# Local attention: values projected over 128 tokens and routed through DRAM as rows

## The chip, the cores and the metric

The kernel runs on one core of one Trainium2 chip. The metric is the device time of one execution in microseconds (us). Inside the core, TensorE (PE) multiplies matrices, VectorE (DVE), ScalarE (ACT) and GpSimd (POOL) work element by element, and SyncE (SP) issues the transfers (DMAs) that 16 DMA engines carry out. The core's on-chip memory has 128 partitions; TensorE writes its results into PSUM, eight banks of 128 x 512 float32.

## The reference, cut to what matters

The program computes two gated blocks on 4 sequences of 1024 tokens with 128 channels. The change touches the last part, six layers of local attention with a feed-forward net behind each:

```python
DIM = 128; DEPTH = 6; HEADS = 16; DIM_HEAD = 64; WINDOW = 32
def attn_layer(x, Wqkv, qs, ksc, Wo):
    q, k, v = jnp.split(x @ Wqkv, 3, -1)          # 16 heads of 64 channels each
    q = l2norm(q) * qs; k = l2norm(k) * ksc
    q, k = rotated and scaled by position
    # the queries of a window of 32 tokens see the keys and the values of
    # their own window and of the one before: 64 tokens, masked to a band
    sim  = einsum('bhwie,bhwje->bhwij', bq, bk2) * 8.0
    out  = einsum('bhwij,bhwje->bhwie', softmax(masked sim), bv2)
    return out @ Wo
for i in range(DEPTH):
    x = attn_layer(shift_tokens(x), ...) + x
    x = ffn_layer(shift_tokens(x), ...) + x
```

All of it is float32. What matters for the change is `bv2`: each window of 32 queries is multiplied with 64 rows of values, the window's own 32 and the 32 ahead of them, so the ranges of 64 tokens overlap by half.

## The kernel before, in words

The tokens of all sequences form 32 tiles of 128 tokens (`NT` = 32, `P` = 128). The function `layers` holds all six layers in one block, in which each engine has its own program and waits on semaphores. `reach(eng, l, sem, n)` waits for the n-th event of layer l.

Each engine walks through the tiles by `steps(...)`: in step n it does the listed pieces of work, each for tile n minus its lateness. On TensorE the order within one step is: queries of tile n (`make_q`, L1610), keys of tile n (`make_k`, L1623), transposed queries of tile n-1 (`turn_q`, L1631), 12 of the 16 output projections of tile n-3 (`project`, L1710), transposed keys of tile n-1 (`turn_k`, L1642), the other 4 projections (`project_rest`), transposed probabilities of tile n-2 (`turn_p`, L1653), scores of tile n-1 (`score`, L1662 for the mask and L1671), values of tile n (`make_v`, L1684) and the weighted sum of values of tile n-2 (`weigh`, L1703). So the values of tile n are used two steps after they are made. Each float32 matmul appears in the trace as two matmuls with two weight loads.

Values before: `make_v` projects each tile in four matmuls, two per half of the tile (64 tokens each), whose results stand in the lower and in the upper 64 columns of the array: the even heads of a token lie in partitions 0 to 63 and the odd ones in partitions 64 to 127. ScalarE copies them to `values` (`out_v`, L1834), two slots per tile in a ring of three tiles (`RING` = 3). That gives the windows that begin at a multiple of 64 tokens. The windows in between are put together in a second ring, `mixed`: SyncE copies blocks of 32 partitions within the on-chip memory, 4 transfers of 128 KB per tile, or 6 where the ring wraps (L1580 to L1585). `weigh` waits for them by `mixes`, then takes `mixed` and `values` in turn, window by window, in matmuls on 64 rows and 64 columns of the array with 32 moving columns.

At the start of the block GpSimd clears two stretches of memory (L2057, L2058), and TensorE and SyncE wait for that. The small weights of the net are fetched at the start of a layer (L1573), those of the next layer's attention at its end (L1592).

Of the kernel before, what the change touches and what calls it, by code (L numbers as in the profile page):

```python
# [8 lines left out]
ACT = mybir.ActivationFunctionType  # L9
AX_X = mybir.AxisListType.X  # L10
F32 = mybir.dt.float32
# [3 lines left out]
P = 128  # L15
# [3 lines left out]
T = B * L  # L19
CH = 512  # L20
NCH = T // CH
NT = T // P
# [20 lines left out]
DH = 64  # L43
INNER = HEADS * DH
PAIRS = HEADS // 2
PAIRS_AHEAD = 6
WIN = 32
# [51 lines left out]
def chunk(c):  # L99
    return slice(c * CH, (c + 1) * CH)  # L100
# [1332 lines left out]


AHEAD_TILES = 3
RING = 3
VALUE_SLOT, SCORE_SLOT, KEY_SLOT, OUT_SLOT = range(4)


# [10 lines left out]
FETCHES, NEXT = 4, 4  # L1450


def layers(nc, ps, k, w, xs, cur, fetches, w1, w2, b1, small, next_fetches):

# [21 lines left out]
    with Stage(nc, "layer") as st:  # L1476
# [7 lines left out]
        prob = st.sb("prob", [P, PAIRS, 2, DH])  # L1484
        prob_t = st.sb("prob_t", [P, PAIRS, P])
        top, total = st.sb("top", [P, HEADS]), st.sb("total", [P, 2, HEADS])
        values = st.sb("values", [P, 2 * RING, PAIRS, DH])
        mixed = st.sb("mixed", [P, 2 * RING, PAIRS, DH])
        heads_out = st.sb("heads_out", [P, PAIRS, P])

        fetched, cleared, mixes = st.sem("fetched"), st.sem("cleared"), [st.sem(f"mixes{r}") for r in range(RING)]
# [13 lines left out]
        two_banks = lambda slot: ps[:, 2 * slot:2 * slot + 2, :]  # L1505
# [28 lines left out]
        for sem, n in (  # L1534
                (fetched, 16 * FETCHES), (next_in, 16 * NEXT), (q_made, NT), (k_made, NT), (v_made, NT), (q_turned, NT),
                (k_turned, NT), (scored, NT), (p_turned, NT), (weighed, NT), (projected, NT), (q_squared, NT), (k_squared, NT),
                (logged, NT), (q_out, NT), (k_out, NT), (raised, NT), (p_out, NT), (o_out, NT), (v_out, NT), (q_parts, 2 * NT),
                (k_parts, 2 * NT), (summed, 2 * NT), (guarded, NT), (inverted, NT), (topped, NT), (shifted, NT), (totalled, NT),
                (evened, NT), (over, NT), (added, NT), (q_rotated, 2 * NT), (k_rotated, 2 * NT), (q_scaled, NT), (k_scaled, NT),
                (lows, 2 * NCH), (ups, 2 * NCH), (turned, NCH), (summed_up, NCH), (centres, NCH), (squared, NCH), (spread, NCH),  # L1540
                (norm_evened, 3), (norm_logged, 3), (norm_inverted, 3), (norm_scaled, NCH), (backs, NCH), (outs, NCH),
                (lefts, len(units)), (gates, len(units)), (gelus, len(units)), (gated, len(units)), (net_summed, len(units)),
                (done, NCH), (roped, 4), *((mixes[r], 16 * (4 if r else 6) * len(range(r, NT, RING))) for r in range(RING))):
            per_layer[id(sem)] = n

        def reach(eng, l, sem, n):

            n += l * per_layer[id(sem)]
            if n > 0:
                eng.wait_ge(sem, n)  # L1550
# [2 lines left out]

            return lambda t: do() if t == NT - 1 else None

        def mix_count(t):
            return 16 * (4 if t % RING else 6) * (t // RING + 1)

        def steps(*plan):
            for n in range(NT + AHEAD_TILES):  # L1560
# [4 lines left out]
        with nc.Block() as block:  # L1565

            @block.sync
            def _(sp):
                sp.wait_ge(cleared, 2)
                for l in range(LAYERS):  # L1570
                    reach(sp, l, done, 0)
                    for dst, src in fetches(l):
                        sp.dma_start(dst, src).then_inc(fetched, 16)  # L1573
                    for t in range(NT):
                        r = t % RING * 2
                        reach(sp, l, v_out, t + 1)
                        reach(sp, l, weighed, t - RING + 1)
                        for lo in (0, DH):
                            a, b = slice(lo, lo + WIN), slice(lo + WIN, lo + DH)
                            sp.dma_start(mixed[b, r:r + 2], values[a, r:r + 2]).then_inc(mixes[t % RING], 16)  # L1580
                            if r:
                                sp.dma_start(mixed[a, r:r + 2], values[b, r - 1:r + 1]).then_inc(mixes[t % RING], 16)
                            else:
                                sp.dma_start(mixed[a, 1], values[b, 0]).then_inc(mixes[t % RING], 16)
                                sp.dma_start(mixed[a, 0], values[b, 2 * RING - 1]).then_inc(mixes[t % RING], 16)  # L1585
                    for t in range(NT - RING, NT):
                        reach(sp, l, mixes[t % RING], mix_count(t))
                    reach(sp, l, fetched, 16 * FETCHES)
                    reach(sp, l, projected, NT)
                    if l + 1 < LAYERS:  # L1590
                        for to, of in next_fetches(l + 1):
                            sp.dma_start(to, of).then_inc(next_in, 16)  # L1592
                        reach(sp, l, next_in, 16 * NEXT)

            @block.tensor
            def _(pe):
# [78 lines left out]
                def make_v(t):  # L1675
                    if t >= 2:
                        reach(pe, l, p_out, t - 1)
                    else:
                        reach(pe, l, q_out, t)
                    if t == 0 and l:  # L1680
                        reach(pe, l, gelus, 0)
                    for a in range(2):
                        for h in range(2):
                            last = nc.tensor.matmul(two_banks(VALUE_SLOT)[h * DH:(h + 1) * DH, a, :],  # L1684
                                                    xs[:, t * P + a * DH:t * P + (a + 1) * DH],
                                                    w["qkv"][:, 2, chunk(h)], start=True, stop=True)
                    last.then_inc(v_made, 1)

                def weigh(t):
                    reach(pe, l, p_out, t + 1)  # L1690
                    reach(pe, l, mixes[t % RING], mix_count(t))
                    if t + 2 < NT:
                        reach(pe, l, k_parts, 2 * t + 6)
                    else:
                        reach(pe, l, o_out, t)
                    for p in range(0, PAIRS, 2):
                        for i in range(P // WIN):
                            src = (mixed, values)[i % 2]
                            for h in range(2):
                                for e in range(2):  # L1700
                                    rows, at = slice(h * DH, (h + 1) * DH), slice(e * DH, (e + 1) * DH)
                                    out = by_pair(KEY_SLOT)[at, h * 4 + p // 2, i * WIN:(i + 1) * WIN]
                                    last = nc.tensor.matmul(out, src[rows, t % RING * 2 + i // 2, p + e, :],  # L1703
                                                            prob_t[rows, p + e, i * WIN:(i + 1) * WIN],
                                                            start=True, stop=True)
                    last.then_inc(weighed, 1)
# [78 lines left out]
            def _(act):  # L1785
# [252 lines left out]
            def _(pool):  # L2038
# [92 lines left out]
def build_program(nc, a, out):  # L2131


    with ExitStack() as whole:
# [3 lines left out]
        def loads(tensors):  # L2138
# [52 lines left out]
        with ExitStack() as ctx:  # L2191
# [7 lines left out]
            def for_attention(layer):  # L2199
# [3 lines left out]
            shift_tokens(nc, cur, xs, w["rope"], w["scales"])  # L2203
            layers(nc, ps, k, w, xs, cur, lambda l: [(t[:], a[n][l]) for n, t in (("w1", w1), ("w2", w2), ("b1", b1),
                                                                                  ("small", small))],
                   w1, w2, b1, small, for_attention)
        gate_and_store(nc, ps, x, s, cur, out)


# [107 lines left out]
```

## Time and profile before

| What | Value |
|---|---|
| median of 3 runs | 4994.56 us (4994.17 to 4994.9) |
| profiled execution | 5013.37 us, of which the span from first to last instruction is 5011.6 us |
| granted TensorE clock, mean | 0.951 of full speed |
| busy share of the span | PE 89%, DVE 74%, ACT 55%, POOL 43% |
| DMA over the span | 204.72 MB, mean 41 GB/s |

A profile shows one execution. Each engine's busy time is the time in which it works on recorded instructions. The span is cut in 40 slices, whose digits show the busy share in tenths. A timeline lists instructions in order of their start; neighbours of one kind are merged, so that a line's time runs to the end of the last of them, and a bracket names the idle time before a line and what ended it. "issue" stands there for a wait for which the trace has no cause.

### The profile page before, as it was taken

How to read it: one execution, taken by the hardware profiler on the slowest of the kernel's cores; microseconds unless marked ns; L12 is line 12 of the kernel's file. 1: busy time of each engine (PE TensorE's matmuls, PEld its weight loads, DVE VectorE, ACT ScalarE, POOL GpSimd, SP SyncE). 2: the span in 40 equal slices, each digit the busy share in tenths (PEclk: the TensorE clock that was granted, in tenths of full speed). 3: DMA queues.
4: the chain of work that ended last, by engine and by line, in shares of the span. 5: the costliest groups of instructions: out<-in, count | busy, mean ns of one | idle time of the engine just before them, and what ended most of it. 6: DMA issues, size and time to landing. Idle time of an engine off the chain costs nothing. (4 is left out here: it accounts for less than half of the span.)

```text
span 5011.6 us, 169931 instructions
## 1 busy us (share of the span) xinstructions
PE 4437.7 (89%) x75610; PEld 2774.2 (55%) x75610; DVE 3689.3 (74%) x4181; ACT 2775.2 (55%) x3767; POOL 2162.7 (43%) x1739
## 2 busy tenths in 40 slices
PE   2876888595898699999999999999999999999998
PEld 1652333363333267765777476756776577646774
DVE  1667887124788488877888688858987799768885
ACT  1644777233677555655665565655655566545664
POOL 1332000313000066645665466636664566546661
PEclk6997999696999899999999999999999999999999
DMA  1002111112011111111111111111111111111110
GB/s 42 1 25 66 39 45 33 60 36 84 25 43 41 54 40 41 41 49 31 41 41 37 44 41 41 41 44 39 41 39 49 36 41 41 38 42 41 39 40 25
DMA packets 108209, 204.72 MB, mean 41 GB/s; under 512 B 28594, under 2 KB 56882, under 8 KB 105650
## 3 DMA queue, kind: packets, MB, share of 16 engines
q1 hardware_dynamic: 105432, 189.65, 14.5%
q8 instruction: 598, 9.80, 0.8%
q0 software_dynamic: 2048, 4.20, 0.3%
q14 instruction: 131, 1.07, 0.1%
HBM read 67.52 MB, written 22.81 MB: 18 GB/s over the span
## 5 line engine op out<-in xcount | busy, mean ns | idle before, releaser
L2044 POOL TENSOR_TENSOR part_of_layer<-part_of_layer,sine_of_layer 128x512 f32<-128x512 f32 x768 | 963.2, 1276 | 620.7 <-DVE sine_of_layer L1920 620.7
L2055 POOL TENSOR_TENSOR part_of_layer<-part_of_layer,inverse_of_layer 128x1024 f32<-128x1024 f32 x384 | 730.1, 1901 | 261.2 <-ACT inverse_of_layer L1803 246.1
L976 ACT ACTIVATE prob_of_ca<-ps 128x1024 f32<-128x1024 f32 (+3 forms) x768 | 591.9, 814 | 245.4 <-PE ps L850 173.0
L1917 DVE TENSOR_TENSOR part_of_layer<-ps,rope 128x1024 f32<-128x1024 f32 x384 | 466.1, 1214 | 33.0 <-ACT square_of_layer L1791 31.4
L1920 DVE TENSOR_TENSOR sine_of_layer<-ps,rope 128x1024 f32<-128x1024 f32 x384 | 464.8, 1210 | 0.0
L1834 ACT ACTIVATE values_of_layer<-ps 128x1024 f32<-128x1024 f32 x192 | 196.5, 1023 | 458.4 <-PE ps L1684 458.4
L868 PE MATMUL ps<-keys_of_ca,queries_of_ca 64*128 64x512 bf16 (+3 forms) x1536 | 325.8, 341 | 133.9 <-DVE top_of_ca L1008 59.7
L1703 PEld LDWEIGHTS ps<-prob_t_of_layer,mixed_of_layer 64*64 64x64 f32 x12288 | 342.4, 135 | 164.1 <-issue 154.5
L1710 PE MATMUL ps<-heads_out_of_layer,wo 128*128 128x128 f32 x3072 | 417.8, 281 | 13.1 <-ACT heads_out_of_layer L1823 12.1
L1956 DVE TENSOR_REDUCE total_of_layer<-prob_of_layer 128x16 f32<-128x1024 f32 x192 | 234.1, 1219 | 237.9 <-ACT prob_of_layer L1827 237.9
L1610 PE MATMUL ps<-qkv,shifted 128*128 128x512 f32 x768 | 383.2, 621 | 24.0 <-POOL values_of_layer L2058 19.9
L1703 PE MATMUL ps<-prob_t_of_layer,mixed_of_layer 64*64 64x32 f32 x12288 | 392.7, 221 | 13.0 <-ACT prob_t_of_layer L1818 6.7
L1703 PE MATMUL ps<-prob_t_of_layer,values_of_layer 64*64 64x32 f32 x12288 | 391.0, 220 | 12.9 <-issue 12.0
L1710 PEld LDWEIGHTS ps<-heads_out_of_layer,wo 128*128 128x128 f32 x3072 | 383.4, 197 | 16.9 <-ACT heads_out_of_layer L1823 16.9
L1684 PE MATMUL ps<-qkv,shifted 128*64 128x512 f32 x1536 | 383.7, 612 | 7.1 <-issue 7.1
L1008 DVE TENSOR_REDUCE top_of_ca<-ps 128x2 f32<-128x1024 f32 (+1 forms) x320 | 357.3, 1117 | 40.2 <-PE ps L868 24.8
L1623 PE MATMUL ps<-qkv,shifted 128*128 128x512 f32 x768 | 362.8, 595 | 12.0 <-DVE sine_of_layer L1920 12.0
L1703 PEld LDWEIGHTS ps<-prob_t_of_layer,values_of_layer 64*64 64x64 f32 x12288 | 345.2, 135 | 18.8 <-issue 17.4
L1813 ACT ACTIVATE keys_of_layer<-ps 128x1024 f32<-128x1024 f32 x192 | 196.8, 1025 | 248.9 <-PE ps L1642 248.9
L919 PE MATMUL ps<-prob_of_ca,values_of_ca 128*32 128x512 f32 (+3 forms) x3072 | 327.2, 498 | 0.7 <-ACT summed_of_ca L962 0.7
L1964 DVE TENSOR_TENSOR prob_of_layer<-prob_of_layer,total_of_layer 128x1024 f32<-128x1024 f32 x192 | 318.4, 1658 | 6.6
L1671 PE MATMUL ps<-keys_of_layer,queries_of_layer 64*32 64x64 f32 x24576 | 298.7, 228 | 4.1 <-issue 3.2
(237 smaller groups left out, 8831.1 us busy)
## 6 DMA issues: line engine op xcount, KB each, us to landing
mixed_of_layer<-values_of_layer SPq DMA_DIRECT2D x636, 128.0 KB
mixed_of_layer<-values_of_layer SPq DMA_DIRECT2D x264, 64.0 KB
queries_of_ca<-q_parts SPq DMA_DIRECT2D x384, 32.0 KB
keys_of_ca<-k_parts SPq DMA_DIRECT2D x384, 32.0 KB
qkv<-in_qkv SPq DMA_DIRECT2D x6, 1536.0 KB, 6.3
q_parts<-parts_of_ci SPq DMA_DIRECT2D x16, 384.0 KB, 2.5
k_parts<-parts_of_ci SPq DMA_DIRECT2D x16, 384.0 KB
rope<-in_rope SPq DMA_DIRECT2D x6, 1024.0 KB, 8.9
```

The source lines that it names most:

```text
L919: last = nc.tensor.matmul(ps[h * QUAD:(h + 1) * QUAD, SUM_BANK, j:], values[:, G % 2, kt, h, :], prob[:, i % 2, h, j:], start=kt == 0, sto ...
L976: nc.scalar.activation(prob[:, i % 2, 2 * two:2 * two + 2, j:], ps[:, 2 * two:2 * two + 2, j:], ACT.Exp, scale=scale).then_inc(raised, 1)
L1008: nc.vector.reduce_max(to, pair[:, :, 0:width], AX_X).then_inc(pair_used, 1)
L1610: last = nc.tensor.matmul(two_banks(SCORE_SLOT)[:, a, :], xs[:, tokens(t)], w["qkv"][:, 0, chunk(a)], start=True, stop=True)
L1623: last = nc.tensor.matmul(two_banks(KEY_SLOT)[:, a, :], xs[:, tokens(t)], w["qkv"][:, 1, chunk(a)], start=True, stop=True)
L1684: last = nc.tensor.matmul(two_banks(VALUE_SLOT)[h * DH:(h + 1) * DH, a, :], xs[:, t * P + a * DH:t * P + (a + 1) * DH], w["qkv"][:, 2, chu ...
L1703: last = nc.tensor.matmul(out, src[rows, t % RING * 2 + i // 2, p + e, :], prob_t[rows, p + e, i * WIN:(i + 1) * WIN], start=True, stop=True)
L1710: last = nc.tensor.matmul(two_banks(OUT_SLOT)[:, 0, 0:P], w["o"][:, p, :], heads_out[:, p, :], start=p == 0, stop=p == PAIRS - 1)
L1917: nc.vector.tensor_tensor(part[:, t % 2, side], by_head(slot), table(2 * side, t), ALU.mult).then_inc(parts, 1)
L1920: nc.vector.tensor_tensor(sine[:, side], by_head(slot), table(2 * side + 1, t), ALU.mult).then_inc(parts, 1)
L2044: nc.gpsimd.tensor_tensor(out, out, sine[:, side, :, (1 - to) * half:(2 - to) * half], ALU.add).then_inc(rotated, 1)
L2055: nc.gpsimd.tensor_tensor(part[:, t % 2, side], part[:, t % 2, side], by, ALU.mult).then_inc(scaled, 1)
```

## The change

`make_v` projects the 128 tokens of a tile at once, in two matmuls with all 128 columns, as `make_k` does. The results (token by row) go to `values`, now two slots of one tile. SyncE writes each tile as 128 rows of 4 KB (512 KB) to a new DRAM tensor `v_rows`, which begins with 32 rows of zeros, waits until it has landed, and then reads the four overlapping ranges of 64 tokens of that tile back, in four transfers of 256 KB (two per parity of the heads, two per parity of the window), into `windows`, a ring of two tiles. `weigh` reads all four windows from there. The matmuls of `weigh` keep their number and shape.

```diff
-RING = 3
+RING = 2
...
-        values = st.sb("values", [P, 2 * RING, PAIRS, DH])
-        mixed = st.sb("mixed", [P, 2 * RING, PAIRS, DH])
+        values = st.sb("values", [P, 2, 2, PAIRS * DH])
+        windows = st.sb("windows", [P, RING, P // WIN, PAIRS, DH])
...
             def _(sp):
                 sp.wait_ge(cleared, 2)
+                sp.dma_start(v_rows[0:WIN, :], values[0:WIN, 1].rearrange("p h n -> p (h n)")).then_inc(padded, 16)
+                sp.wait_ge(padded, 16)
...
                     for t in range(NT):
-                        r = t % RING * 2
                         reach(sp, l, v_out, t + 1)
+                        sp.dma_start(v_rows[WIN + t * P:WIN + (t + 1) * P, :], values[:, t % 2].rearrange("p h n -> p (h n)"))\
+                            .then_inc(stored[t % 2], 16)
+                        reach(sp, l, stored[t % 2], stores(t))
                         reach(sp, l, weighed, t - RING + 1)
-                        for lo in (0, DH):
-                            a, b = slice(lo, lo + WIN), slice(lo + WIN, lo + DH)
-                            sp.dma_start(mixed[b, r:r + 2], values[a, r:r + 2]).then_inc(mixes[t % RING], 16)
-                            if r:
-                                sp.dma_start(mixed[a, r:r + 2], values[b, r - 1:r + 1]).then_inc(mixes[t % RING], 16)
-                            else:
-                                sp.dma_start(mixed[a, 1], values[b, 0]).then_inc(mixes[t % RING], 16)
-                                sp.dma_start(mixed[a, 0], values[b, 2 * RING - 1]).then_inc(mixes[t % RING], 16)
+                        for h in range(2):
+                            for odd in range(2):
+                                of = v_rows[t * P + odd * WIN:(t + 1) * P + odd * WIN, h * CH:(h + 1) * CH]
+                                sp.dma_start(windows[h * DH:(h + 1) * DH, t % RING, odd::2].rearrange("r a p d -> r a (p d)"),
+                                             of.rearrange("(a r) n -> r a n", r=DH)).then_inc(windowed[t % RING], 16)
...
-                    for a in range(2):
-                        for h in range(2):
-                            last = nc.tensor.matmul(two_banks(VALUE_SLOT)[h * DH:(h + 1) * DH, a, :],
-                                                    xs[:, t * P + a * DH:t * P + (a + 1) * DH],
-                                                    w["qkv"][:, 2, chunk(h)], start=True, stop=True)
+                    for h in range(2):
+                        last = nc.tensor.matmul(two_banks(VALUE_SLOT)[:, h, :], xs[:, tokens(t)],
+                                                w["qkv"][:, 2, chunk(h)], start=True, stop=True)
                     last.then_inc(v_made, 1)
...
-                    reach(pe, l, mixes[t % RING], mix_count(t))
+                    reach(pe, l, windowed[t % RING], window_count(t))
...
-                            src = (mixed, values)[i % 2]
...
-                                    last = nc.tensor.matmul(out, src[rows, t % RING * 2 + i // 2, p + e, :],
+                                    last = nc.tensor.matmul(out, windows[rows, t % RING, i, p + e, :],
...
                 def out_v(t):
                     reach(act, l, v_made, t + 1)
-                    reach(act, l, weighed, t - RING + 1)
-                    if t >= RING - 1:
-                        reach(act, l, mixes[(t + 1) % RING], mix_count(t - RING + 1))
-                    nc.scalar.activation(values[:, t % RING * 2:t % RING * 2 + 2], by_head(VALUE_SLOT).rearrange(
-                        "p (a h) d -> p a h d", a=2), ACT.Copy).then_inc(v_out, 1)
+                    if t < 2:
+                        act.wait_ge(padded, 16)
+                    if t >= 2 or l:
+                        reach(act, l, stored[t % 2], stores(t - 2))
+                    nc.scalar.activation(values[:, t % 2], two_banks(VALUE_SLOT), ACT.Copy).then_inc(v_out, 1)
...
-                nc.gpsimd.memset(values[:, 2 * RING - 1], 0.0).then_inc(cleared, 1)
+                nc.gpsimd.memset(values[:, 1], 0.0).then_inc(cleared, 1)
...
+        v_rows = nc.dram_tensor("v_rows", [WIN + T, INNER], F32).ap()
```

## Rows read from the trace of the kernel before

**Rows 1.** The page: TensorE's busy share and granted clock in 40 slices.

```profile
PE   2876888595898699999999999999999999999998
...
PEclk6997999696999899999999999999999999999999
```

**Rows 2.** Windows: stretch, then busy us (instructions) per engine, granted clock, DMA share, GB/s.

```profile
2300.00:2740.00 440.00, 429.17 (x9805) 304.77 (x9813) 386.34 (x369) 260.75 (x317) 292.10 (x226) 0.99 0.18 41
...
3390.00:3830.00 440.00, 431.15 (x9919) 306.97 (x9915) 389.36 (x372) 261.54 (x315) 285.16 (x220) 1.00 0.17 40
```

**Rows 3.** Timeline of PE, one step: start us, us, engine, line, instructions.

```profile
2012.63 1.99 PE L1610 MATMUL ps<-qkv,shifted 128*128 128x512 f32 x4
2014.46 1.88 PE L1623 MATMUL ps<-qkv,shifted 128*128 128x512 f32 x4
2016.17 1.04 PE L1631 MATMUL ps<-sb_ident,part_of_layer 128*128 128x128 f32 x8
...
2021.01 1.49 PE L1671 MATMUL ps<-keys_of_layer,queries_of_layer 64*32 64x64 f32 x128
2022.42 1.94 PE L1684 MATMUL ps<-qkv,shifted 128*64 128x512 f32 x8
2024.29 0.32 PE L1703 MATMUL ps<-prob_t_of_layer,mixed_of_layer 64*64 64x32 f32 x8
...
2026.29 1.98 PE L1610 MATMUL ps<-qkv,shifted 128*128 128x512 f32 x4
```

**Rows 4.** Timeline of PE: the longest stalls inside a step.

```profile
4306.34 1.48 PE L1671 MATMUL ps<-keys_of_layer,queries_of_layer 64*32 64x64 f32 x128
4309.35 1.94 PE L1684 MATMUL ps<-qkv,shifted 128*64 128x512 f32 x8 [1.53 <-issue]
```

**Rows 5.** The page: DMA queues with packets, MB, share of 16 engines.

```profile
q1 hardware_dynamic: 105432, 189.65, 14.5%
q8 instruction: 598, 9.80, 0.8%
```

**Rows 6.** Timeline of PE's weight loads (PEld): values, then queries.

```profile
2008.69 0.20 PEld L1684 LDWEIGHTS ps<-qkv,shifted 128*64 128x64 f32 x4
2009.17 0.14 PEld L1684 LDWEIGHTS ps<-qkv,shifted 128*64 128x64 f32 x2 [0.29 <-issue]
2009.60 0.14 PEld L1684 LDWEIGHTS ps<-qkv,shifted 128*64 128x64 f32 x2 [0.29 <-issue]
2010.56 0.21 PEld L1703 LDWEIGHTS ps<-prob_t_of_layer,mixed_of_layer 64*64 64x64 f32 x8 [0.81 <-issue]
...
2012.63 0.30 PEld L1610 LDWEIGHTS ps<-qkv,shifted 128*128 128x128 f32 x2
2013.17 0.19 PEld L1610 LDWEIGHTS ps<-qkv,shifted 128*128 128x128 f32 x1 [0.24 <-issue]
```

**Rows 7.** Timeline of SP's queue: the issues of one tile.

```profile
2012.92 0.59 SPq L1585 DMA_DIRECT2D mixed_of_layer<-values_of_layer  x1
2013.55 0.59 SPq L1580 DMA_DIRECT2D mixed_of_layer<-values_of_layer  x1
```

**Rows 8.** DMA issues: operation, count, KB each, median us from issue to landing.

```profile
qkv<-in_qkv SPq DMA_DIRECT2D x6, 1536.0 KB, 6.3
q_parts<-parts_of_ci SPq DMA_DIRECT2D x16, 384.0 KB, 2.5
rope<-in_rope SPq DMA_DIRECT2D x6, 1024.0 KB, 8.9
```

**Rows 9.** Timelines of ACT and PE: the last tile of a layer.

```profile
2191.99 1.02 ACT L1834 ACTIVATE values_of_layer<-ps 128x1024 f32<-128x1024 f32 x1 [2.23 <-PE ps L1684]
...
2212.94 0.32 PE L1703 MATMUL ps<-prob_t_of_layer,mixed_of_layer 64*64 64x32 f32 x8 [1.11 <-ACT prob_t_of_layer L1818]
```

**Rows 10.** Windows: loads from DRAM, then the `mixed` transfers of one tile.

```profile
2219.00:2229.00 10.00, 8.55 (x31) 4.50 (x32) 5.55 (x9) 6.57 (x10) 2.77 (x4) 1.00 0.83 321
2011.70:2017.50 5.80, 5.80 (x85) 3.80 (x78) 4.62 (x5) 4.12 (x5) 4.15 (x3) 1.00 0.36 82
```

**Rows 11.** Timelines of POOL and PE: the start of the layers.

```profile
1746.18 0.52 POOL L2058 MEMSET values_of_layer<- 128x512 f32 x1
...
1746.76 3.78 PE L1610 MATMUL ps<-qkv,shifted 128*128 128x512 f32 x4 [19.89 <-POOL values_of_layer L2058]
```

More of the change, by code:

```diff
@@ L1450, with layers @@
 FETCHES, NEXT = 4, 4
-def layers(nc, ps, k, w, xs, cur, fetches, w1, w2, b1, small, next_fetches):
+def layers(nc, ps, k, w, xs, cur, fetches, w1, w2, b1, small, next_fetches, v_rows):
     units = [(c, f) for c in range(NCH) for f in range(NCHUNKS)]
@@ L1486, in layers @@
         top, total = st.sb("top", [P, HEADS]), st.sb("total", [P, 2, HEADS])
-        values = st.sb("values", [P, 2 * RING, PAIRS, DH])
-        mixed = st.sb("mixed", [P, 2 * RING, PAIRS, DH])
+        values = st.sb("values", [P, 2, 2, PAIRS * DH])
+        windows = st.sb("windows", [P, RING, P // WIN, PAIRS, DH])
         heads_out = st.sb("heads_out", [P, PAIRS, P])
-        fetched, cleared, mixes = st.sem("fetched"), st.sem("cleared"), [st.sem(f"mixes{r}") for r in range(RING)]
+        fetched, cleared, padded = st.sem("fetched"), st.sem("cleared"), st.sem("padded")
+        stored, windowed = [st.sem(f"stored{r}") for r in range(2)], [st.sem(f"windowed{r}") for r in range(RING)]
         q_made, k_made, v_made = st.sem("q_made"), st.sem("k_made"), st.sem("v_made")
@@ L1542, in layers @@
                 (lefts, len(units)), (gates, len(units)), (gelus, len(units)), (gated, len(units)), (net_summed, len(units)),
-                (done, NCH), (roped, 4), *((mixes[r], 16 * (4 if r else 6) * len(range(r, NT, RING))) for r in range(RING))):
+                (done, NCH), (roped, 4), *((stored[r], 16 * NT // 2) for r in range(2)),
+                *((windowed[r], 16 * 4 * len(range(r, NT, RING))) for r in range(RING))):
             per_layer[id(sem)] = n
@@ L1554, in last, with stores, window_count @@
             return lambda t: do() if t == NT - 1 else None
-        def mix_count(t):
-            return 16 * (4 if t % RING else 6) * (t // RING + 1)
+        def stores(t):
+            return 16 * (t // 2 + 1)
+        def window_count(t):
+            return 16 * 4 * (t // RING + 1)
         def steps(*plan):
@@ L1574, in _ @@
                     for t in range(NT):
-                        r = t % RING * 2
                         reach(sp, l, v_out, t + 1)
+                        sp.dma_start(v_rows[WIN + t * P:WIN + (t + 1) * P, :], values[:, t % 2].rearrange("p h n -> p (h n)"))\
+                            .then_inc(stored[t % 2], 16)
+                        reach(sp, l, stored[t % 2], stores(t))
                         reach(sp, l, weighed, t - RING + 1)
-                        for lo in (0, DH):
-                            a, b = slice(lo, lo + WIN), slice(lo + WIN, lo + DH)
-                            sp.dma_start(mixed[b, r:r + 2], values[a, r:r + 2]).then_inc(mixes[t % RING], 16)
-                            if r:
-                                sp.dma_start(mixed[a, r:r + 2], values[b, r - 1:r + 1]).then_inc(mixes[t % RING], 16)
-                            else:
-                                sp.dma_start(mixed[a, 1], values[b, 0]).then_inc(mixes[t % RING], 16)
-                                sp.dma_start(mixed[a, 0], values[b, 2 * RING - 1]).then_inc(mixes[t % RING], 16)
+                        for h in range(2):
[3 more added lines that the diff above has]
+                                             of.rearrange("(a r) n -> r a n", r=DH)).then_inc(windowed[t % RING], 16)
                     for t in range(NT - RING, NT):
-                        reach(sp, l, mixes[t % RING], mix_count(t))
+                        reach(sp, l, windowed[t % RING], window_count(t))
                     reach(sp, l, fetched, 16 * FETCHES)
@@ L2205, in build_program @@
                                                                                   ("small", small))],
-                   w1, w2, b1, small, for_attention)
+                   w1, w2, b1, small, for_attention, v_rows)
         gate_and_store(nc, ps, x, s, cur, out)
```

## The prediction

> **What bounds the kernel now.** I read the page first, for who is busy and where. From about slice 15 on, the six layers, TensorE stands at 9 in almost every slice, at nearly full granted clock [rows 1]. Next come the windows of single layers: in 440 us TensorE is busy 429 to 431 us, VectorE 386 to 389 us, the DMA engines 17 to 18% of the time [rows 2]. So TensorE sets the pace of these 3,200 us, with VectorE at 88% behind it, and transfers have room. The number of matmuls gives the length of a step: the listed loops make 320 recorded matmuls per tile (8 for queries and keys, 24 for the transposes, 16 projections, 8 for the mask, 128 scores, 8 values, 128 weighing), so 9,805 to 9,919 in 440 us are 30.6 to 31.0 tiles, 14.2 to 14.4 us each.
>
> The timeline of TensorE shows one step from inside. From one start of L1610 to the next it takes 13.66 us, and each group begins when the one before lets it [rows 3]. Nothing in it waits for values. What separates the usual 14.2 to 14.4 us from 13.66 us are stalls such as the 1.53 us after a block of scores, which the trace puts down to no engine ("issue") [rows 4]. About 0.6 us per tile, 192 tiles: 115 us in all. TensorE's instructions come by DMA too: 598 packets of 9.80 MB on the queue marked instruction [rows 5], 16.4 KB each, which is one for 250 or so of the 151,220 matmuls and weight loads, 2.5 per tile. They are what I suspect behind these stalls.
>
> **The value projection on TensorE.** Before, it costs 1.87 us from its start to the start of L1703, 192 times [rows 3]. The loads show the inside [rows 6]: the first pair of half-width matmuls takes 0.48 us (2008.69 to 2009.17), the next ones 0.43 us each, and the last pair, which begins one interval after 2009.60, gives way to L1703 only after 0.53 us, at 2010.56. Two half-width matmuls run side by side, so that four of them cost no more streaming time than two of full width: halving the count saves nothing there. What differs is entry and exit. The full-width queries, which too follow a group of small matmuls, pay 0.54 us for the first matmul (2012.63 to 2013.17), since a load of 128 columns takes 0.19 us where one of 64 takes 0.14 us, and then 0.43 us each. The exit stays: L1703 still has another array shape. The sum after is 0.54 + 0.43 + 0.43 + 0.53 = 1.93 us, against 1.87 us: +0.06 us from these rounded rows. I take 0.055 us x 192 = **+10.5 us**. Bounds: down to -29 us if the values then cost what the keys cost between two full-width groups, 1.71 us [rows 3] ((1.71 - 1.87) x 192 = -31 us, taken as the end), and up to +16 us if draining 128 columns takes 0.03 us more than draining 64 (half of the 0.06 us by which entries differ).
>
> The Trainium skill says the same of the exit in TensorEngine Tiling (Array Packing), section Key Properties: changing the tiling mode drains the array. By it the 0.10 us at the exit remain with full-width values, and -29 us is out of reach; the trace agrees in that both switches next to the values cost something, 0.05 and 0.10 us.
>
> Does TensorE's extra time reach the end? Its step is a chain without idle time [rows 3], and the work that hangs on the values (ScalarE's copy, the exponentials behind it, VectorE's sums) starts from the same moment as `weigh` and moves along. So all of it counts. The 8 fewer entries of 640 in TensorE's stream also cut 1% of its instruction packets: -1 us of 115 us of stalls.
>
> **The transfers.** Removed per tile: 4 or 6 issues of 0.59 us on SyncE [rows 7], 512 KB. Added: one store of 512 KB, a wait for it, four reads of 256 KB; 1.5 MB together. By rows: a store of 384 KB lands 2.5 us after its issue [rows 8], so 512 KB in some 2.8 us; then four issues of about 0.6 us [rows 7], the last at 2.8 + 1.8 = 4.6 us, and at most 6.3 us for it, the time of a load of 1.5 MB, or 8.9 us, that of 1 MB behind 2 MB of others [rows 8]. The windows of a tile are there 11 to 13.5 us after its copy. They are needed two steps later, 26 us in the middle of a layer; the shortest notice is the last tile's, from 2193.01 (2191.99 + 1.02) to 2212.94, 19.9 us [rows 9]. Margin: over 6 us at the worst point. SyncE itself is held for 2.8 + 2.4 = 5.2 us of 13.7 us. Behind its new wait stand only the same tile's reads and the next tile's store, which comes a step later; `weighed` of tile t-2 is done at about the time at which tile t's values are copied, before the store lands. ScalarE's new wait is for the store of two tiles ago. The cover is 6 us wide; if it were gone, every microsecond beyond would be paid on `weigh`, at first once per layer.
>
> Capacity: loads from DRAM ran at 321 GB/s with the engines 83% busy, the on-chip `mixed` transfers at 82 GB/s with 36% [rows 10]; per full share that is 387 and 228 GB/s. So 1.57 MB take 4.1 to 6.9 us of each step, a share of 0.30 to 0.50 after 0.17. No bound, but instruction packets share the engines. Their mean time now is 0.8% x 16 x 5011.6 us / 598 = 1.07 us [rows 5]. If a packet is held in proportion to the added share (0.13 to 0.33), it is 0.14 to 0.35 us late. TensorE runs through instructions fast only in the scores and in weighing, and of a step the new transfers cover the time from the copy to 8 to 11 us on; the copy of the tile in [rows 3] ends at about 2022.42 + 1.94 + 1.02 = 2025.4, the next scores begin one step after 2021.01, at 2034.7, 9 us later. So I see a part of one packet per tile touched, a tenth of the stall time at 0.14 us: 192 x 0.1 x 0.14 = 3 us. Bounds: 0, if no packet that TensorE waits for meets a read, and 27 us, if one in each tile does. I take **+3 us**.
>
> The Trainium skill, in Runtime: NRT & Kernel Launch, section Instruction fetch mechanics, has the fetches "mostly hidden". By it this term would be 0; the stalls of [rows 4] speak against that here.
>
> **The start.** GpSimd clears 1,024 elements per partition in place of 512, which took 0.52 us, and TensorE waits for it [rows 11]: **+0.5 us**. SyncE's write of the zeros and the wait for it (under 3 us by the 2.5 us above) lie ahead of small loads that the net needs only at the layer's end, and ScalarE's first copy of values waits for TensorE's first projections, of which the queries alone take 3.78 us there [rows 11]: nothing.
>
> **Sum.** 10.5 + 3 + 0.5 - 1 = +13 us on the profiled execution's 5013.37 us, 0.26%. That execution is 18.8 us above the median of the runs (4994.56 us); the added work is the same in both. So 4994.56 + 13: **5007.5 us**. Rounding to 0.01 us alone moves the main term by 2 us either way.
>
> **The rivals.**
> 1. *No change that can be measured* (within 0.2%, 10 us, about what a measurement of this kernel can tell from no change). The same mechanism with the entry at 0.04 us or less and untouched packets: +5 to +9 us, 5002 us. For it: the rows' second digit. Against it: three of the four terms are positive. Chance 0.34 for all sums from -10 to +10 us.
> 2. *Instruction packets held by the reads.* The bytes triple, and the stalls are real [rows 4]. If each tile has one packet 0.14 us late on top of the main term: +27 + 10 = 5032 us; at 0.35 us, 5070 us. Against it: most of the new traffic lies under long matmuls, and `mixed` was slower per byte. Chance 0.14.
> 3. *Faster: the switch costs vanish.* If the 0.10 us at the exit belong to the half-width form and not to L1703's, values cost 0.54 + 3 x 0.43 = 1.83 us, the queries' price: (1.83 - 1.87) x 192 = -8 us; with the keys' 1.71 us, 4966 us. It decides for faster once the values cost less than 1.81 us. Chance 0.08.
> 4. *The windows come late.* If write, wait and read took over 20 us, each layer's end would be held, over 26 us every tile; at 30 us 4 us for each second tile or so, some 384 us, 5380 us. Rows give 13.5 us at most. Chance 0.03.
> 5. The forecast, +10 to +25 us: 0.41.
>
> **How the numbers follow.** Slower by over 0.2% (above 5004.5 us): forecast, packets and late windows, 0.41 + 0.14 + 0.03 = 0.58. Same: 0.34. Faster: 0.08. The range leaves out rival 3 below -8 us and, above, the upper half of rival 2 and rival 4: 4987 to 5030 us. The likeliest case alone: 5004.5 to 5020 us.
>
> **What would show it.** In the changed profile, the step from the start of the value projection to L1703 should be 1.91 to 1.94 us, with 4 matmuls of 128*128; the waits of L1703 should name no DMA; a tile's last read should land within 14 us of the copy; the DMA share of a layer should be 0.30 to 0.50; and the issue stalls before L1671, L1684 and L1703 should keep their sums within 20 us. The prediction is wrong if the value group takes 1.83 us or less, if stalls grow by 30 us or more, or if `weigh` is seen waiting for `windows`.

## The result, and the profile after

The changed kernel takes 5271.82 us (median of 4 runs, 5256.11 to 5283.99) against 4994.73 us (median of 4): a ratio of 1.055, 95% interval 1.052 to 1.0581, or 277 us more. The profiled execution took 5256.11 us with a span of 5254.3 us, 243 us more than the profiled execution of before (5013.37 us). The forecast was +13 us.

The page of the changed kernel: TensorE's busy share and granted clock, the DMA engines' share, and the queues (compare [rows 1] and [rows 5]).

```profile
PE   2977887777897799889999899999999899899998
...
PEclk6998998787999899999999999999999999999998
DMA  1011111112111444424342344324342344423431
...
q1 hardware_dynamic: 200520, 391.11, 28.1%
q8 instruction: 592, 9.70, 0.8%
```

TensorE is no longer at 9 in every slice of the layers. DMA bytes doubled, and the engines' share went from 14.5% to 28.1%. The same 430 us of the first layer, which hold steps alone in both kernels, before and then after (columns as in [rows 2]):

```profile
1760.00:2190.00 430.00, 419.12 (x9610) 297.20 (x9608) 381.49 (x364) 255.88 (x310) 286.71 (x224) 1.00 0.18 41
```

```profile
1760.00:2190.00 430.00, 395.49 (x8813) 283.20 (x8813) 342.23 (x333) 232.79 (x282) 258.17 (x201) 0.97 0.41 104
```

TensorE is busy 24 us less, at a mean granted clock of 0.97 after 1.00. With 320 recorded matmuls per tile before and 316 after, the step has grown from 14.3 to 15.4 us.

The timeline of all engines shows where the time goes, in one step (start us, us, engine, line; the bracket is idle time and its end):

```profile
2017.89 2.53 SPq L1590 DMA_DIRECT2D windows_of_layer<-v_rows  x4
...
2022.58 1.40 PE L1677 MATMUL ps<-keys_of_layer,queries_of_layer 64*32 64x64 f32 x118
...
2026.94 0.45 PE L1677 MATMUL ps<-keys_of_layer,queries_of_layer 64*32 64x64 f32 x10 [2.96 <-issue]
...
2027.32 3.78 PE L1689 MATMUL ps<-qkv,shifted 128*128 128x512 f32 x4
...
2031.13 1.02 ACT L1838 ACTIVATE values_of_layer<-ps 128x1024 f32<-128x1024 f32 x1 [7.38 <-PE ps L1689]
```

After 118 of 128 score matmuls TensorE stops for 2.96 us, though it needs no new data: the other ten belong to the same group. Then the value projection takes 3.78 us in place of the 1.98 us that four matmuls of this shape take at full clock [rows 3]. The windows of single microseconds around it show both reasons (busy us per engine, granted clock, DMA share, GB/s; a DMA packet is counted where it starts, so that a share can be over 1):

```profile
2020.00:2021.00 1.00, 1.00 (x12) 1.00 (x11) 1.00 (x2) 0.00 (x0) 1.00 (x1) 1.00 1.10 279
2021.00:2022.00 1.00, 1.00 (x11) 1.00 (x11) 1.00 (x2) 0.97 (x1) 1.00 (x2) 1.00 1.06 199
2022.00:2023.00 1.00, 1.00 (x52) 0.60 (x53) 1.00 (x2) 0.70 (x2) 0.69 (x2) 1.00 1.07 229
2023.00:2024.00 1.00, 0.98 (x92) 0.82 (x84) 1.00 (x2) 0.72 (x3) 0.10 (x1) 1.00 1.04 199
2024.00:2025.00 1.00, 0.00 (x0) 0.00 (x0) 0.29 (x1) 0.00 (x0) 1.00 (x1) 1.00 0.18 31
2025.00:2026.00 1.00, 0.00 (x0) 0.00 (x0) 0.00 (x0) 0.00 (x0) 1.00 (x2) 1.00 0.00 0
2026.00:2027.00 1.00, 0.06 (x5) 0.06 (x10) 0.00 (x0) 0.00 (x0) 1.00 (x2) 0.62 0.00 0
2027.00:2028.00 1.00, 1.00 (x11) 0.64 (x12) 0.54 (x1) 0.00 (x0) 1.00 (x2) 0.50 0.00 0
```

From 2020 to 2024 the DMA engines are full with the four reads. In the microsecond in which they end, 31 KB move, then nothing. The DMA queues show what came behind the reads (packets, MB, share of 16 engines), first for 2014.90 to 2024.20, then for 2024.20 to 2024.24:

```profile
q1 hardware_dynamic: 634, 1.24, 57.0%
q14 instruction: 1, 0.01, 0.4%
```

```profile
q8 instruction: 1, 0.02, 228.0%
q1 hardware_dynamic: 4, 0.00, 11.1%
```

q8 brings TensorE's instructions: before, 598 packets for 151,220 matmuls and weight loads [rows 5], now 592 for 149,684, and 1,536 fewer entries in 6 fewer packets are 256 per packet (the last experiment, which takes back the projection alone, has 598 packets again). In the first stretch, 9.3 us long, none of its packets starts. The next one starts at the moment at which the reads end. It takes 228% x 16 x 0.04 = 1.46 us, until 2025.7, and TensorE goes on at 2026.94, 1.3 us behind it and 2.7 us after the reads ended.

This is no single case. The trace's packet records, set beside TensorE's matmuls, have 87 stalls of over 1 us inside a group of scores or of weighing. Each ends 1.05 to 1.55 us (median 1.41 us) after an instruction packet has ended, and in 68 of the 87 that packet started when at most 20 of the 512 pieces of the tile's reads had still to start. In the other runs, and in the one such stall of the kernel before, the time from the packet's end is 1.2 to 1.8 us. When a packet is asked for, the trace does not tell.

Within the 3 us of idle time the granted clock goes to the lower level (0.5 is 1.2 GHz), at 2026.2, and it stays there for 13.7 us: the matmuls that follow run at half rate.

Over the whole execution, the list of waits (engine, line, what it waited for: us in total, times, longest) has

```profile
PE ps L1677 <- issue: 166.7, 86, 3.1
...
PE ps L1706 <- issue: 38.6, 45, 3.1
```

Before, the same two lines read 3.2 us in 10 waits and 17.6 us in 36:

```profile
PE ps L1703 <- issue: 17.6, 36, 1.1
...
PE ps L1671 <- issue: 3.2, 10, 0.5
```

So 184.5 us of new idle time stand in plain sight in scores and weighing. Both lists are of profiled executions, which differ by 243 us, so 58 us are left. The clock can hold them: its mean over the execution is 0.936 after 0.951, and (1 - 0.936) x 5254.3 - (1 - 0.951) x 5011.6 = 91 us of full-rate work, a part of which falls into the idle time itself.

### The profile page after: what moved, and what is told of

Its sections match the earlier page's. It is cut to its first block and busy times, and to the rows that moved or that the text cites. A ratio compares the mean times of both kernels' runs of the same rounds, so it can differ in the third digit from the quotient of the medians.

```text
span 5254.3 us, 168459 instructions
## 1 busy us (share of the span) xinstructions
PE 4510.1 (86%) x74842; PEld 2845.4 (54%) x74842; DVE 3662.7 (70%) x4181; ACT 2775.7 (53%) x3767; POOL 2149.7 (41%) x1739
## 3 DMA queue, kind: packets, MB, share of 16 engines
q1 hardware_dynamic: 200520, 391.11, 28.1%
## 5 line engine op out<-in xcount | busy, mean ns | idle before, releaser
L1706 PEld LDWEIGHTS ps<-prob_t_of_layer,windows_of_layer 64*64 64x64 f32 x24576 | 401.7, 139 | 204.4 <-issue 194.9
L1706 PE MATMUL ps<-prob_t_of_layer,windows_of_layer 64*64 64x32 f32 x24576 | 429.7, 223 | 46.2 <-issue 38.6
L1677 PE MATMUL ps<-keys_of_layer,queries_of_layer 64*32 64x64 f32 x24576 | 313.6, 229 | 166.7 <-issue 166.7
L1689 PE MATMUL ps<-qkv,shifted 128*128 128x512 f32 x768 | 429.5, 686 | 7.9 <-issue 7.9
L1616 PE MATMUL ps<-qkv,shifted 128*128 128x512 f32 x768 | 390.6, 631 | 25.8 <-POOL values_of_layer L2061 20.8
L1946 DVE TENSOR_REDUCE top_of_layer<-ps 128x16 f32<-128x1024 f32 x192 | 235.0, 1224 | 228.3 <-PE ps L1677 228.3
L1677 PEld LDWEIGHTS ps<-keys_of_layer,queries_of_layer 64*32 64x32 f32 x24576 | 266.3, 107 | 223.6 <-issue 223.3
L1629 PE MATMUL ps<-qkv,shifted 128*128 128x512 f32 x768 | 364.2, 597 | 14.9 <-DVE sine_of_layer L1923 14.9
L1967 DVE TENSOR_TENSOR prob_of_layer<-prob_of_layer,total_of_layer 128x1024 f32<-128x1024 f32 x192 | 282.7, 1472 | 6.6
```

The lines of the kernel that those rows point to most:

```text
L1616: last = nc.tensor.matmul(two_banks(SCORE_SLOT)[:, a, :], xs[:, tokens(t)], w["qkv"][:, 0, chunk(a)], start=True, stop=True)
L1629: last = nc.tensor.matmul(two_banks(KEY_SLOT)[:, a, :], xs[:, tokens(t)], w["qkv"][:, 1, chunk(a)], start=True, stop=True)
L1677: last = nc.tensor.matmul(out, queries[rows, p, i * WIN:(i + 1) * WIN], keys[rows, p, first:first + DH], start=False, stop=p == PAIRS - 1)
L1689: last = nc.tensor.matmul(two_banks(VALUE_SLOT)[:, h, :], xs[:, tokens(t)], w["qkv"][:, 2, chunk(h)], start=True, stop=True)
L1706: last = nc.tensor.matmul(out, windows[rows, t % RING, i, p + e, :], prob_t[rows, p + e, i * WIN:(i + 1) * WIN], start=True, stop=True)
```

## The experiments

Theory A: TensorE's instruction packets stand behind the window reads on the DMA engines, and what it costs depends on where in the step the traffic lies. The rivals: B, the full-width projection disturbs TensorE; C, the new waits cost; D, the added bytes slow the core wherever they lie. Each ratio is to the kernel before, run on the same chip; there the kernel before took 5023.8 us beside the first four experiments and 5016.9 and 5010.9 us beside the others (medians). The changed kernel was not run again beside them; the last experiment, at 1.0564, comes nearest to it. The edits are shown shortened.

### The projection alone

```diff
 kernel before
-  matmul(two_banks(VALUE_SLOT)[h * DH:(h + 1) * DH, a, :], xs[:, t * P + a * DH:t * P + (a + 1) * DH], ...)  # x4
+  matmul(two_banks(VALUE_SLOT)[:, h, :], xs[:, tokens(t)], w["qkv"][:, 2, chunk(h)])                         # x2
```

> The kernel before with the full-width value projection alone (two matmuls with 128 columns in place of four with 64); the values then stand in another order than the weighing takes them for, so the attention output is another one. Theory A (TensorE's instruction packets stand behind the window reads on the DMA engines): this part costs only what the prediction gave it, about +10 us, 5005 us (5000 to 5012), and the granted clock in the layers stays near 1.0. Theory B (the wider projection itself disturbs TensorE's pace or clock): most of the 277 us appears here, over 5150 us.

Measured: 0.9981 (0.9967 to 0.9994), 5008.77 us against 5023.8. B is out. The projection's own step came out as forecast. Its timeline of weight loads:

```profile
2003.96 0.30 PEld L1683 LDWEIGHTS ps<-qkv,shifted 128*128 128x128 f32 x2
2004.50 0.19 PEld L1683 LDWEIGHTS ps<-qkv,shifted 128*128 128x128 f32 x1 [0.24 <-issue]
2004.92 0.19 PEld L1683 LDWEIGHTS ps<-qkv,shifted 128*128 128x128 f32 x1 [0.24 <-issue]
2005.87 0.21 PEld L1701 LDWEIGHTS ps<-prob_t_of_layer,mixed_of_layer 64*64 64x64 f32 x8 [0.76 <-issue]
```

From the start to the weighing it takes 1.91 us. That is the 0.54 us for the first matmul that the prediction took from the queries, and the exit of 0.52 us. Still the kernel is 9.5 us faster by the ratio (3 to 17 us by its interval; the medians lie 15 us apart) and not 10 us slower. Something else gives back some 20 us. TensorE's idle time ahead of the weighing fell only from 17.6 to 16.2 us in the list of waits, and no view accounts for the whole.

### Small reads, early reads, late transfers

```diff
 tiny_reads: changed kernel
+  n = CH if l == 0 and t < RING else 16       # values read per row
 early_reads: changed kernel
+  for t in range(NT):
+      wait for v_out of t; if t: read(t - 1)  # waits stored, weighed; four reads
+      store(t)
+  read(NT - 1)
 late_mixes: kernel before
+  reach(sp, l, k_out, t + 1)                  # ahead of the on-chip transfers
```

> The changed kernel, with the reads of the windows cut to 16 of 512 values per row after the first two tiles (same number of transfers, same waits; the weighing works on old windows). Theory A: without the bulk of the reads the stalls go back to the level of before, 5000 to 5020 us. Theory B: stays near 5270 us. Theory C (the new chain of waits on SyncE, ScalarE or TensorE is what costs, not the bytes): stays above 5200 us, because every wait is kept and a small transfer still takes its 2 us.

> The changed kernel with the same bytes and transfers, but the reads of a tile issued when the next tile's values have been copied, ahead of that tile's store, so that they run while TensorE is in the long query and key matmuls, not ahead of the scores. Theory A: most of the loss goes, since few instruction packets are asked for then: 5000 to 5080 us. Theory B: near 5270 us. Theory C: the windows come a step later and the margin shrinks, so if waits were the matter it gets slower than 5270 us. Theory D (the added bytes slow TensorE wherever they lie, by contention in the memory): near 5270 us.

> The kernel before, nothing changed but the moment of its on-chip transfers: SyncE issues them only when the next step's keys have been copied, some 9 us later, when the scores begin. Theory A: their 5 us of queued transfers now stand before the packets that scores and weighing need, so this kernel too gets slower by 100 us or more, with issue stalls before L1671 and L1703 of 2 us and more. Theories B, C and D: no more than 20 us, since neither the projection nor the bytes nor the number of waits on a late transfer change.

Measured: small reads 0.9983 (0.9973 to 0.9992); early reads 1.0003 (0.9994 to 1.0012); late on-chip transfers in the kernel before 1.0108 (1.0093 to 1.0124).

C falls with the small reads: all waits stand, the loss is gone. D falls with the early reads: all bytes stand, the loss is gone. The microseconds of early_reads show the same full engines, but before the scores:

```profile
2017.00:2018.00 1.00, 1.00 (x12) 1.00 (x10) 1.00 (x2) 0.99 (x2) 0.00 (x0) 1.00 1.14 229
2018.00:2019.00 1.00, 1.00 (x12) 1.00 (x11) 1.00 (x2) 0.00 (x0) 0.97 (x1) 1.00 0.97 358
2019.00:2020.00 1.00, 1.00 (x11) 1.00 (x11) 1.00 (x2) 0.86 (x1) 1.00 (x2) 1.00 0.35 131
2020.00:2021.00 1.00, 1.00 (x45) 0.60 (x44) 1.00 (x2) 0.70 (x2) 0.79 (x2) 1.00 0.04 8
2021.00:2022.00 1.00, 1.00 (x108) 0.93 (x85) 1.00 (x2) 0.83 (x3) 0.00 (x0) 1.00 0.00 0
```

The reads went out with the copy of the next tile's values, at 2011.36 (SyncE's queue), and all traffic ends in 2019 to 2020, 8 us later. The scores (45 and 108 instructions in a microsecond) run without a break at full clock. Over the execution, the waits before them on "issue" are 13.5 us, against 166.7 us in the changed kernel.

The late transfers show the effect in the kernel before, without a byte added or a matmul changed: 52 us, half of the 100 us that I expected, and before the weighing (33 us more waits than before) instead of the scores, with single stalls of at most 1.7 us where I expected 2 us and more.

```profile
PE ps L1704 <- issue: 51.0, 103, 1.7
```

Its 512 KB are issued one transfer at a time at 0.6 us each, from the scores on, so that by theory A it is the packets for the weighing that wait, and each for less.

### The store or the reads, wide pieces, pairs, and a version without DRAM

```diff
 tiny_store: changed kernel, from layer 2 on
+  n = INNER if l == 0 else 16                 # values stored per row
 wide_reads: changed kernel
+  dma_start(windows[:, t % RING, 2 * h + odd], 128 rows of v_rows)
 paced_reads: changed kernel, after the first two reads
+  reach(sp, l, windowed[t % RING], window_count(t) - 32)
 direct: full-width projection, no store; per tile and half h, windows[h * DH + to ...] from values
+  for to, i, of, src, n in ((0, 1, 0, now, 64), (0, 3, 64, now, 64), (0, 2, 32, now, 64),
+                            (0, 0, 96, past, 32), (32, 0, 0, now, 32)):
```

> The changed kernel, whose store is cut to 16 of 1024 values per row from the second layer on; the four reads keep all their bytes (layers 2 to 6 weigh old values for the rest). It separates the store from the reads. Theory A (instruction packets stand behind the reads): the loss stays, ratio to before 1.04 to 1.06; the reads begin about 1 us earlier in a step, so it may move by some 0.5% either way. If the store is what holds the packets, the ratio falls to 1.00 to 1.01 as with the small reads.

> The changed kernel with reads of the same bytes, the same count and the same 2 KB pieces, but each spread over all 128 partitions in place of 64 (the rows land in other places than the weighing takes them for). Theory A with a queue of fixed length in pieces: the same 512 pieces at the same 155 ns each hold the packets as long, ratio 1.04 to 1.06. Theory A with slow pieces because only half the partitions are written at a time: pieces take about 85 ns, as those of the scales and biases did, the queue drains in under 3 us instead of 5.2, before the packets for the scores are asked for, and the ratio falls below 1.02.

> The changed kernel with one more wait: SyncE issues the last two reads of a tile only when the first two have landed. Bytes and transfers stay. Theory A: no packet stands behind more than two reads, some 2.6 us in place of up to 5.2, and the gap between the pairs lets a waiting packet through: single stalls fall from over 3 us to under 1.5 us and the ratio to 1.01 to 1.03. Theory C (waits on SyncE cost): slower than 1.055, since a wait is added and the windows land later. Against A would be a ratio still at 1.05.

> A version that might beat both: the full-width projection of the changed kernel, but no DRAM. Ten on-chip transfers per tile (64 or 32 partitions, 2 KB pieces, 1 MB together) bring the windows straight from the values of this tile and the one before, issued right after the copy of the values. The issues alone take 10 x 0.59 = 5.9 us, so the traffic lies from 0.6 to about 7 us after the copy, under the long query and key matmuls and mostly ahead of the packets that scores need. Theory A: like the full-width projection alone, 0.998, up to 1.003 if the tail of the traffic meets packets. If the bytes count wherever they lie, it is slower than 1.01.

Measured: small store 1.0192 (1.0176 to 1.0208); wide reads 1.002 (1.0011 to 1.003); pairs 1.0297 (1.0279 to 1.0314); direct 0.9997 (0.9988 to 1.0006), 5014.15 us.

The small store leaves stalls of the known kind, so the reads make them without it, but fewer of them. In its first layer, where the store is still whole, and in the other five the waits are

```profile
PE ps L1678 <- issue: 27.8, 14, 2.8
```

```profile
PE ps L1678 <- issue: 65.9, 71, 2.5
```

which is 28 us in one layer and 13 us in each of the others (the changed kernel has 29.6 us in its first and 27 us in each of the others). The ratio fell by 3.6%, not by the 0.5% that I allowed: without the bulk of the store half of the stalls go. What the traces show is that the reads moved, and by little. SyncE's queue in the fourth layer, small store first, changed kernel behind it:

```profile
3515.74 0.33 SPq L1584 DMA_DIRECT2D v_rows<-values_of_layer  x1
3518.36 2.53 SPq L1591 DMA_DIRECT2D windows_of_layer<-v_rows  x4
```

```profile
3539.27 0.33 SPq L1583 DMA_DIRECT2D v_rows<-values_of_layer  x1
3543.77 2.54 SPq L1590 DMA_DIRECT2D windows_of_layer<-v_rows  x4
```

From the second layer on the reads go out 2.0 us behind the small store and 3.7 us behind the whole one (medians of 160 tiles). One or two microseconds in the step decide; that the missing bytes of the store do nothing else is argued and not shown.

The wide reads carry the same bytes in the same 2 KB pieces and lose almost nothing. Their engines move more at less share:

```profile
2025.00:2026.00 1.00, 1.00 (x5) 0.47 (x4) 0.99 (x2) 0.34 (x1) 0.00 (x0) 1.00 0.69 250
2026.00:2027.00 1.00, 1.00 (x11) 1.00 (x10) 1.00 (x2) 0.96 (x2) 0.00 (x0) 1.00 0.89 275
2027.00:2028.00 1.00, 1.00 (x11) 1.00 (x11) 1.00 (x2) 0.98 (x2) 0.19 (x1) 1.00 0.95 268
2028.00:2029.00 1.00, 1.00 (x11) 1.00 (x11) 1.00 (x2) 0.00 (x0) 1.00 (x1) 1.00 0.63 234
```

1027 / 3.16 = 325 GB/s per full share in these four microseconds, against 906 / 4.27 = 212 GB/s from 2020 to 2024 in the changed kernel. Over all reads of the layers a 2 KB piece takes 148 ns in the changed kernel and 100 ns here (means): transfers into 64 partitions at a time hold the engines half as long again, and with 128 the queue is mostly empty before the scores. These rows land in other places than the weighing takes them for, so this run is a test and no repair.

Pairs: single stalls fell from 3.1 to 1.9 us, but the added landing carries the last two reads on into the weighing, where the stalls now are (89.0 us in 101 waits, with 24.1 us in 31 left before the scores). I had expected single stalls under 1.5 us; the ratio of 1.03 is the upper end of what A gave it; C, which wanted over 1.055, is wrong again.

The version without DRAM is as fast as the kernel before and no faster. Neither it nor early_reads beats the kernel before, and I ran no other repair.

### Half the reads, reads after the scores, and the number of instructions

```diff
 half_reads: changed kernel
+  n = CH if h == 0 or l == 0 and t < RING else 16
 late_reads: changed kernel, ahead of the reads
+  reach(sp, l, scored, t + 1)
 half_v: changed kernel, value projection for a in range(2), tokens a * 64 to a * 64 + 63
+  matmul(two_banks(VALUE_SLOT)[a * DH:(a + 1) * DH, h, :], ...)
```

> The changed kernel with the two reads of one half of the partitions in full and the other two cut to 16 of 512 values per row after the first two tiles (old values are weighed for that half). Half the queue: theory A puts the end of the traffic at 8 to 9 us after the copy instead of 11, so that packets asked for later pass; as the cost depends on when in the step the queue ends, less than half of it stays: ratio 1.00 to 1.02. A cost proportional to the bytes would give 1.027.

> The changed kernel, with the four reads issued only after the scores of the next step (about 11 us after the copy of the values). Bytes and count stay. The traffic then lies under the weighing and the next queries, and the packets that are asked for between the scores and the weighing stand behind it. Theory A: stalls of 2 to 3 us move from the scores to the weighing, ratio 1.03 to 1.07. If only the scores were sensitive: near 1.00. If waits or the landing time mattered, this should be the slowest of all, for the windows now land some 17 us after the copy.

> The changed kernel with the value projection back in four half-width matmuls (same rows in the same places), all transfers as changed. TensorE's stream has 645 entries per tile again in place of 637. By the projection's own price alone (0.047 us per tile longer at full width, some stalls fewer) the ratio stays within 0.003 of 1.055. If the loss rests on how many packets per tile fall due (637 entries are close to two and a half packets, so that the same collision comes back in every second tile for a whole layer), it moves by over 1% here, most likely down to 1.03 to 1.045.

Measured: half the reads 1.0 (0.999 to 1.001); reads after the scores 1.0083 (1.0067 to 1.01); half-width projection 1.0564 (1.0511 to 1.0616).

Half of the read bytes cost nothing at all, not half of the loss: the cost goes by where the queue ends and is no price per byte. The packet records give the place, as the median start of a tile's last read piece, counted from the start of the next scores (layers 2 to 6):

| run | last read piece | ratio |
|---|---|---|
| half the reads | 1.8 us before | 1.000 |
| wide reads | 0.9 us before | 1.002 |
| small store | 0.6 us before | 1.019 |
| changed kernel | 0.8 us after | 1.055 |
| half-width projection | 0.8 us after | 1.056 |

The reads after the scores did less harm than the 1.03 that I took as the least. They are the last to land and not the slowest, which speaks against C once more. The wait let them go when the value projection begins, 1.7 us before the weighing (2025.29 and 2027.01), and most of their traffic lies under the long projections; the weighing's stalls rise to 33.2 us only. So, of the places tried, the most sensitive is the one in which the reads of the changed kernel end, at the start of the scores. The half-width projection changed nothing: my guess that 637 entries per tile, near two and a half packets, bring the same collision back is wrong, and the projection has no part in the loss.

## Why the prediction was wrong

- *What bounds the kernel*: right. TensorE sets the pace, and its stalls on "issue" are what grew. The 115 us that I gave these stalls before are not in the list of waits, which has 32 us of them for TensorE's matmuls.
- *The value projection, +10.5 us*: the step was right, 1.92 us after 1.87 us. The sum was not: alone, the part gives -9.5 us. No run shows where the other 20 us come from, or whether the term for 1% fewer entries, -1 us, is the one that was too small.
- *The transfers are hidden from `weigh`*: right. No wait of L1706 names a transfer of the windows. In the step shown the reads end at 2024.2, some 11 us after the copy; I had 11 to 13.5 us.
- *Capacity, 4.1 to 6.9 us of each step*: right as a sum. In the step shown the store holds the engines for 1.3 us and the four reads for 4.8 us (2019.4 to 2024.2), and the share of the first layer is 0.41, within 0.30 to 0.50. But the reads run at 212 GB/s per full share, below both rates that I had taken as ends [rows 10], and so as one block of 5 us: none of the transfers that I compared wrote from DRAM into half of the partitions.
- *Instruction packets, +3 us, at most 27 us*: **this is the step that failed.** I let a packet be late "in proportion to the added share", 0.14 to 0.35 us. In the runs the packet starts when the queued reads have ended, and TensorE goes on 2.7 us later, so that the delay goes by what is left of the queue (5 us), not by the share: 184.5 us of new stalls in place of 3 us. I also took the meeting of reads and scores for rare, a tenth of a packet per tile, with traffic to 8 to 11 us after the copy, though my own sum had the windows there only at 11 to 13.5 us and the scores from 9 us on; in the median tile the last read piece starts 0.8 us after the scores. And I had no term for the clock that falls during a stall of 3 us.
- *Rival 2* named the mechanism and the place, and priced it at 5032 to 5070 us, with a chance of 0.14. Its price was wrong by the same step.
- *What would show it*: of the signs named, one spoke. The stalls grew by 184.5 us where 30 us was the limit; the value group, the landing and the DMA share came out as forecast.

The Trainium skill, in Runtime: NRT & Kernel Launch, section Instruction fetch mechanics, calls the fetches mostly hidden; this case's trace does not agree for a TensorE stream with 128 matmuls in 1.5 us, with 86 stalls before the scores and 166.7 us in them.

That it is the packets which stand behind the reads is shown by the packets themselves, which start as the reads end and land 1.05 to 1.55 us before TensorE goes on, and by position (early, late, half, wide, small reads, and the kernel before with late transfers). What stays open is how far ahead a packet is asked for, which would turn the map of sensitive places into a rule, and why the full-width projection alone is faster. How much of the loss is the clock alone was not separated by a run.

## What to carry to other kernels

Where TensorE runs through hundreds of small matmuls, its instructions are traffic too: look for "issue" stalls inside a group of matmuls, and price a new transfer by how long the whole queue keeps the DMA engines full and where in the loop that time ends, not by bytes or by its own deadline. The same megabyte and a half cost 5.5% when its queue ended 11 us behind a copy of values and nothing when it ended 8 us behind one. Let transfers write all 128 partitions where the layout allows it: that alone took the ratio from 1.055 to 1.002. To see whether a stall is a late instruction packet, ask for the DMA queues in a narrow window before its end.

## What the runs showed of the hardware

- Reads of 2 KB pieces from DRAM into 64 partitions took 148 ns per piece, into 128 partitions 100 ns (means); in single steps they moved 212 and 325 GB/s per full share of the DMA engines.
- An instruction packet for TensorE held 256 matmuls and weight loads (1,536 fewer entries, 6 fewer packets). In 87 stalls of over 1 us TensorE went on 1.05 to 1.55 us after such a packet had ended.
- In the step shown, TensorE's stall began while the DMA engines were full (at 2023.98) and ended 2.7 us after the last read (2024.2 to 2026.94).
- During 3 us of idle time the granted clock fell from 1.00 to 0.50, stayed there for 13.7 us, and four matmuls took 3.78 us in place of 1.98 us.
- The same kernel before took 4994.7 us beside the changed kernel, 5016.9 and 5010.9 us in two series on the chip of the later experiments, and 5023.8 us on the chip of the first four.
